# A graph layer on one core: edge attributes laid out by attribute, the first filter layer as two row-tiled matmuls, its bias on ACT

## The chip, the cores and the metric

One core of a Trainium2 chip. Times are device microseconds (us) of one execution; the kernel before is given as the median of three runs. Engine names are those of the profile: PE (TensorE, with PEld for its weight loads), DVE (VectorE), ACT (ScalarE), POOL (GpSimd), SP (SyncE, which here only starts transfers).

## The reference

A message-passing layer over 6250 nodes of 128 features and 200,000 edges sorted by `dst`, each edge with 20 attributes and one cutoff:

```python
h = jnp.maximum(_layernorm(x, axis=-1), 0.0)
xw = h @ W_in
W_ij = shifted_softplus(edge_attr @ W_f1 + b_f1) @ W_f2 + b_f2      # 200000 x 128
x_ij = xw[dst] * (W_ij * cutoff)
out  = segment_sum(x_ij, src, 6250)
x + shifted_softplus(out @ W_o1 + b_o1) @ W_o2 + b_o2
```

All of it is float32; `shifted_softplus(z)` is `softplus(z) - log 2`. In the reference, `src` picks the row that a message is added to and `dst` the row that is gathered.

## The kernel before

**Three stages.** A setup (to 146 us) normalizes the nodes, multiplies them by `W_in`, stores the product in three bf16-exact parts, turns the edge lists into the forms that the loop needs, and decides by two measured maxima which of two loops runs. Here that is the "hybrid" one. The edge loop (146 to about 2535 us) runs over 391 chunks of 512 edges. A last stage (about 100 us) adds up accumulators and computes the output layers. The change touches setup and loop.

**One chunk of the loop.** The 512 edges of a chunk are 4 tiles (T) of 128.

1. SP loads the chunk's attributes (128 partitions of 4 edges x 20 numbers), its row of `dst`, its row of `src`, and a window of 42 node rows (`xwin`). Each has four buffers.
2. PE transposes the attributes (line 1283) into `ps[0]`, and ACT copies them to `attrT` (line 756), whose row 80 is all ones.
3. PE multiplies with four copies of `W_f1`, each placed at the 20 rows of one tile with `b_f1` as row 81 and zeros elsewhere: four matmuls of 128 columns (line 1288, `hidden_product`) into `hidden_ps`, one PSUM bank.
4. ACT computes Abs, Exp and Ln (lines 719, 721, 723, `softplus`), DVE adds max(z, 0) (line 1026, `combine`), which signals `s_h`, hidden ready.
5. PE gathers the node rows by a one-hot product (line 1351); ACT scales them by the cutoff (line 749); PE runs the second filter layer (lines 1293, 1295); DVE multiplies the two into the message (line 1082).
6. The messages are added to nodes in one of two ways. In a turn of 16 chunks, chunks 3, 7, 11 and 15 are "on PE": their messages are put in 16 bins by 8 groups of four matmuls (`bin_up`, line 1316), each group emptied from one PSUM bank by ACT (`take_binned`, line 732) before the next may start, and later added by 48 half-height matmuls (`add_nodes`, line 1331). The other 12 are "pool chunks": PE sums equal `src` within a tile (`same_product`, line 1302), ACT empties the four sums (line 765), DVE makes targets (lines 1017, 1021), and POOL starts four adding scatters (line 606).

**What sets the order.** Every engine runs its queue in the order written; `hybrid_steps` calls each engine's `step(u, k)` for k = 0 to 15 of turn u. In step k, PE does: hidden(k+1); the first of two `bin_up` groups; gather and filter of chunk k; the transpose for k+2; in two steps of four `add_nodes` (`DENSE_AT`); the other `bin_up`; the sums of chunk k-1. ACT does: softplus(k+1); the first `take_binned`; the four scalings of k; the `attrT` copy for k+2; the other `take_binned`; the sums of k-1. `BINNED_AT` spreads the 8 groups of a PE chunk over the following steps, two in each step. So there are three kinds of step, by k mod 4: 1 and 3 ("plain": sums and no `add_nodes`), 2 (both) and 0 (`add_nodes` and no sums, since chunk k-1 was on PE).

Waits that matter here: hidden(k+1) waits for `attrT` and for hidden(k) ready; `bin_up` waits for the `take_binned` before it; the sums wait for the `attrT` copy, because both use `ps[0]`.

**Setup.** The edge lists are loaded as 391 rows of 512 integers, `cutoff` as floats. POOL casts `src` and `dst` to float (line 586) and `src` to int16 with the order of its elements changed (line 589). PE turns `src` and `cutoff` into columns by 32 transposes (line 1234, `column`), which ACT copies to `src_col` and `cut_col` (line 681). They stand ahead of the node blocks in PE's queue (`tr`, line 1210; `product`, line 1220). SP stores the parts (line 480) and clears the accumulators between them (line 464).

## Time and profile before

| | us |
|---|---|
| median of 3 runs (lowest to highest) | 2643.63 (2637.69 to 2644.58) |
| the profiled execution | 2637.52 |
| its span | 2635.6 |
| busy in the span: PE, PEld | 2334.9 (89%), 1729.0 (66%) |
| busy in the span: DVE, ACT, POOL | 1842.1 (70%), 1721.8 (65%), 1914.4 (73%) |
| mean granted TensorE clock | 0.968 of full speed |

The busy time of an engine is the union of its instructions. A matmul's record lasts longer than the time until the next matmul may start, so in a timeline the distance from one group's start to the next group's start is what the group costs, and the group's own length is when its result is there. A float32 matmul shows as two records ("x8" is four matmuls).

### The profile page before, as it was taken

To read this page: it belongs to the slowest core of one execution; us is meant where nothing else is said; L and a number is where in the kernel's file an instruction comes from. 1 tells how busy PE (TensorE), PEld (TensorE's weight loads), DVE (VectorE), ACT (ScalarE), POOL (GpSimd) and SP (SyncE) were. 2 spreads that over 40 slices of the span, in tenths; PEclk is the share of its full clock that TensorE was granted. 3 is DMA by queue.
4 is the path that set the end of the run, shared out by engine and by line. 5 is a ranking of instruction groups with operands and counts; after the bars stand their busy time and mean duration, and the time that the engine had idled before them with its cause. 6 is when DMAs were issued, how large, how long until landed. Compare 5 with 4: busy or idle time off the path is not lost.

```text
span 2635.6 us, 71554 instructions
## 1 busy us (share of the span) xinstructions
PE 2334.9 (89%) x19063; PEld 1729.0 (66%) x19063; DVE 1842.1 (70%) x4064; ACT 1721.8 (65%) x4279; POOL 1914.4 (73%) x1235
## 2 busy tenths in 40 slices
PE   3369999999999999999999999999999999999946
PEld 2247776776766677676676676676776676777724
DVE  7546777776777677676777777776677677777658
ACT  2147777776677677676777777677676777777713
POOL 2038887777777777877777787787777777777753
PEclk8579999999999999999999999999999999999967
DMA  7646555655655555555555555555555655555565
GB/s 261 188 78 97 91 90 88 92 87 88 91 87 87 89 90 86 88 92 86 87 88 90 86 90 90 86 88 88 89 87 88 91 87 88 88 90 88 84 140 173
DMA packets 436508, 259.95 MB, mean 99 GB/s; under 512 B 90238, under 2 KB 430181, under 8 KB 436233
## 3 DMA queue, kind: packets, MB, share of 16 engines
q0 software_dynamic: 170976, 80.61, 33.2%
q1 hardware_dynamic: 264121, 176.39, 25.0%
q14 instruction: 243, 1.99, 0.3%
q8 instruction: 32, 0.52, 0.1%
q10 hardware_dynamic: 1136, 0.44, 0.1%
HBM read 153.24 MB, written 104.04 MB: 98 GB/s over the span
## 4 chain that ended last, share of the span: by engine, by line
PE 59%; ACT 17%; issue 11%; DVE 4%; DMA 4%; ACTq 2%; POOL 2%; SPq 1%; DVEq 0%; POOLq 0%
PE ps L1331 13%; PE ps L1316 12%; PE ps L1288 12%; PE ps L1302 11%; PE ps L1295 6%; ACT region L721 5%; ACT region L749 5%; ACT region L719 5%; DMA acc<-region,target 2%; ACT region L732 2%; PE ps L1351 2%; PE ps L1293 1%; POOL acc L606 1%; ACTq L749 1%; ACTq L323 1%
## 5 line engine op out<-in xcount | busy, mean ns | idle before, releaser
L606 POOL DMA_INDIRECT acc<-region,target x1180 | 1863.9, 1580 | 640.1 <-issue 303.7
L1316 PE MATMUL ps<-region 128*128 128x386 bf16 x3072 | 660.9, 336 | 59.9 <-ACT region L732 46.1
L732 ACT ACTIVATE region<-ps 128x386 bf16<-128x386 f32 x768 | 372.9, 486 | 272.7 <-PE ps L1316 267.6
L1026 DVE SCALAR_TENSOR_TENSOR region<-ps,region 128x512 f32<-128x512 f32 x391 | 270.2, 691 | 375.4 <-ACT region L723 311.0
L1316 PEld LDWEIGHTS ps<-region 128*128 128x128 bf16 x3072 | 268.1, 98 | 293.7 <-ACT region L732 86.6
L749 ACT ACTIVATE region<-ps,cut_col 128x128 f32<-128x128 f32 x1564 | 442.7, 372 | 0.0
L1331 PE MATMUL ps<-region 64*128 64x392 bf16 x4608 | 418.5, 328 | 11.9 <-DVE region L1107 11.9
L1288 PE MATMUL ps<-attrT,w_f 81*128 81x128 f32 x3128 | 417.8, 276 | 12.1 <-ACT attrT L756 9.4
L1295 PEld LDWEIGHTS ps<-w_f,region 128*128 128x128 f32 x3128 | 411.3, 192 | 11.2
L1295 PE MATMUL ps<-w_f,region 128*128 128x128 f32 x3128 | 412.4, 275 | 0.0
L1288 PEld LDWEIGHTS ps<-attrT,w_f 81*128 81x128 f32 x3128 | 386.4, 192 | 27.7 <-ACT attrT L756 22.2
L1302 PEld LDWEIGHTS ps<-region 128*128 128x128 f32 x2360 | 291.8, 190 | 156.0 <-issue 79.8
L1302 PE MATMUL ps<-region 128*128 128x129 f32 x2360 | 330.8, 282 | 69.9 <-ACT attrT L756 37.3
L765 ACT ACTIVATE region<-ps 128x516 f32<-128x516 f32 x295 | 177.1, 600 | 266.8 <-PE ps L1302 146.9
L1331 PEld LDWEIGHTS ps<-region 64*128 64x128 bf16 x4608 | 208.7, 94 | 182.5 <-issue 37.0
L719 ACT ACTIVATE region<-ps 128x512 f32<-128x512 f32 x391 | 233.5, 597 | 128.3 <-PE ps L1288 58.0
L1107 DVE TENSOR_SCALAR region<-counting,region 128x392 bf16<-128x392 f16 x768 | 272.8, 395 | 0.0
L723 ACT ACTIVATE region<-region 128x512 f32<-128x512 f32 x391 | 246.2, 630 | 12.4
L721 ACT ACTIVATE region<-region 128x512 f32<-128x512 f32 x391 | 246.2, 630 | 12.3
L1082 DVE TENSOR_TENSOR region<-ps,region 128x512 f32<-128x512 f32 x295 | 203.0, 688 | 36.7 <-ACT region L749 32.2
L1017 DVE TENSOR_SCALAR moved<-region,weight_limit,spare_row 128x4 f32<-128x4 f32 x295 | 86.4, 293 | 195.8 <-ACT region L765 129.5
L1010 DVE TENSOR_TENSOR region<-src_b,src_col 128x512 f32<-128x512 int16 x295 | 201.2, 682 | 0.0
(129 smaller groups left out, 1990.7 us busy)
## 6 DMA issues: line engine op xcount, KB each, us to landing
dst_b<-dst_rows SPq DMA_DIRECT2D x391, 128.0 KB
src_b<-src_rows SPq DMA_DIRECT2D x295, 128.0 KB
xwin<-xw_parts SPq DMA_DIRECT2D x391, 63.0 KB
acc<-region,target POOLq DMA_INDIRECT x1180
attr<-in_edge_attr_dram SPq DMA_DIRECT2D x391, 40.0 KB
acc<-region SPq DMA_DIRECT2D x20, 640.0 KB, 5.1
region<-acc SPq DMA_DIRECT2D x64, 192.0 KB, 3.5
xw_parts<-parts SPq DMA_DIRECT2D x36, 256.0 KB, 3.2
```

The costliest lines, as they stand in the source:

```text
L606: nc.gpsimd.indirect_dma_start(out=acc[t], out_offset=bass.IndirectOffsetOnAxis(ap=target[:, slot, t:t + 1], axis=0), in_=summed[:, slot, ...
L719: nc.scalar.activation(a, z, ACT.Abs).then_inc(steps[0], 1)
L721: nc.scalar.activation(a, a, ACT.Exp, scale=-1.0).then_inc(steps[1], 1)
L732: nc.scalar.activation(binned[:, h, j, :], binned_ps[:, 0:PC], ACT.Copy).then_inc(s_binned, 1)
L749: last = nc.scalar.activation(xg[:, n % 2, t * F:(t + 1) * F], ps[3][:, t * F:(t + 1) * F], ACT.Copy, scale=cut_col[:, bass.ds(u * U + n, ...
L1026: V.scalar_tensor_tensor(hidden[:, odd, :], hidden_ps, 0.0, hidden_exp[:, odd, :], ALU.max, ALU.add).then_inc(s_h, 1)
L1107: V.tensor_scalar(in_node[:, i, slot, :], counting[:, 0:NL], binned[:, slot, j, 3 * F:3 * F + 1], binned[:, slot, j, 3 * F + 1:PC], ALU.su ...
L1288: ins = MM(hidden_ps[:, t * P:(t + 1) * P], w_f1[:, t, :], attrT[0:KA + 1, odd, :], start=True, stop=True)
L1295: ins = MM(ps[2][:, t * F:(t + 1) * F], hidden[:, odd, t * P:(t + 1) * P], w_f2[:, :], start=False, stop=(t == T - 1), skip_group_check=True)
L1302: ins = MM(sums_ps[:, t // 2, t % 2 * FW:(t % 2 + 1) * FW], same[:, odd, t * P:(t + 1) * P], message[:, odd, t, :], start=True, stop=True)
L1316: ins = MM(binned_ps[:, 0:PC], place[:, h % 2, t, j * P:(j + 1) * P], payload_high[:, h % 2, t, :], start=(t == 0), stop=(t == T - 1))
L1331: ins = MM(ps[6 + r][:, 0:NL], binned[rows, slot, j, part * F:(part + 1) * F], in_node[rows, i, slot, :], start=(d == ages[0] and part == ...
```

## The change

`edge_attr` reaches the chip as `(391, 2, 20, 256)`: for each chunk and each half of it, 20 rows of 256 edges. The loop loads it in two transfers, rows 0 to 19 and rows 64 to 83 of one buffer, and multiplies it from there. The transpose and the `attrT` copy are gone. The first filter layer is two matmuls of 256 columns, one on rows 0 to 19, one on rows 64 to 83, into two PSUM banks (4 and 5). The bias comes in by ACT's Abs (`bias=`) and DVE's `combine`; the constant that this leaves is added to the second layer's bias.

Bank 5 now holds half of the hidden layer and the fourth of the sums; the other three sums lie in bank 0 and the binned group moves to bank 1. So the fourth sum's matmul waits for hidden(k+1) to be ready, ACT empties the sums in two instructions, the fourth first, and hidden(k+2) waits for that first one. In PE's queue the first `bin_up` of a step is moved ahead of hidden(k+1).

`src` and `cutoff` also come as columns; `dst`, `src` are laid out so that an edge's place in a chunk is tile by tile, and the copies that changed the order become plain ones. The 200,000 edges are padded to 391 chunks (the last edge repeated with cutoff 0) in place of a last chunk that overlapped.

PE's queue in the loop, from the filter of a step with k mod 4 = 3 to the hidden product of the next. Names: `attrT_ready` is the `attrT` copy, `hidden_ready` `combine`, `binned_ready` `take_binned`, `sums_ready` the emptied sums. Before:

```order
L1293 MATMUL ps<-bf_parts,ones_bf 128x512 [waits message_ready,hidden_ready]
L1295 MATMUL ps<-w_f,region 128x128 x4
L1283 MATMUL ps<-ident,attr 80x128 [waits sums_ready,attrT_ready,attr_loaded1]
L1316 MATMUL ps<-region 128x386 [waits binned_ready,places_ready,payload_ready]
L1316 MATMUL ps<-region 128x386 x3
L1302 MATMUL ps<-region 128x129 [waits sums_ready,attrT_ready,message_ready,same_ready]
L1302 MATMUL ps<-region 128x129 x3
L1288 MATMUL ps<-attrT,w_f 128x128 [waits hidden_ready,attrT_ready]
L1288 MATMUL ps<-attrT,w_f 128x128 x3
L1316 MATMUL ps<-region 128x386 [waits binned_ready]
L1316 MATMUL ps<-region 128x386 x3
```

The same place after (L1236, L1238 filter; L1259 `bin_up`; L1245 sums; L1231 hidden):

```order
L1236 MATMUL ps<-bf_parts,ones_bf 128x512 [waits message_ready,hidden_ready]
L1238 MATMUL ps<-w_f,region 128x128 x4
L1259 MATMUL ps<-region 128x386 [waits binned_ready,places_ready_odd,payload_ready]
L1259 MATMUL ps<-region 128x386 x3
L1245 MATMUL ps<-region 128x129 [waits sums_ready,message_ready,same_ready]
L1245 MATMUL ps<-region 128x129 x2
L1245 MATMUL ps<-region 128x129 [waits hidden_ready]
L1259 MATMUL ps<-region 128x386 [waits binned_ready]
L1259 MATMUL ps<-region 128x386 x3
L1231 MATMUL ps<-attrT,w_f 128x256 [waits last_sums_ready,hidden_ready,attr_loaded1]
L1231 MATMUL ps<-attrT,w_f 128x256
```

The transpose is gone, the sums no longer wait for an `attrT` copy, and a `bin_up` group that stood behind the hidden product stands ahead of it, with a new wait (`last_sums_ready`) on the hidden product.

ACT's queue over the end of a plain step before (L756 `attrT`, L732 `take_binned`, L765 sums, L719 Abs of the next step):

```order
L749 ACTIVATE region<-ps,cut_col 128x128 x3
L756 ACTIVATE attrT<-ps 80x128 [waits hidden_in_psum,attrT_in_psum]
L732 ACTIVATE region<-ps 128x386 [waits binned_in_psum]
L765 ACTIVATE region<-ps 128x516 [waits scattered2,scattered3,scattered1,moved_ready,scattered0,sums_in_psum]
L719 ACTIVATE region<-ps 128x512 [waits hidden_ready,hidden_in_psum]
```

and after:

```order
L728 ACTIVATE region<-ps,cut_col 128x128 x3
L711 ACTIVATE region<-ps 128x386 [waits binned_in_psum]
L701 ACTIVATE region<-ps 128x129 [waits scattered2,scattered3,scattered1,moved_ready,scattered0,sums_in_psum]
L702 ACTIVATE region<-ps 128x387
L693 ACTIVATE region<-ps,bf 128x512 [waits hidden_ready,hidden_in_psum]
```

One instruction is gone from every step and one is added where there are sums.

The diff, cut to its core (the second, "general" loop is changed in the same way and does not run here):

```diff
+    NCH, HALVES, RBF, HALF = attr_cols.shape
-        w_f1 = sb("w_f1", [KA + 1, T, F])
+        w_f1 = sb("w_f1", [64 + RBF, F])
+        attrT = sb("attrT", [64 + RBF, 4, CE // 2])
-        attrT = sb("attrT", [96, 2, P])
-        attrT_ps, hidden_ps = ps[0], ps[4]
-        sums_ps = ps_all[:, 0:2, P:P + 2 * FW]
-        binned_ps = ps[5]
+        hidden_ps = ps_all[:, 4:6, 0:CE // 2]
+        sums_ps = [ps[0][:, t * FW:(t + 1) * FW] for t in range(T - 1)] + [ps[5][:, CE // 2:CE // 2 + FW]]
+        binned_ps = ps[1]
...
+            sp.dma_start(src_int, src_cols).then_inc(s_cols, 16)
+            sp.dma_start(cut_col[:, :, :], cutoff_cols).then_inc(s_cut, 16)
+            def load_attr(c, slot):
+                for r in range(2):
+                    sp.dma_start(attrT[64 * r:64 * r + RBF, slot, :],
+                                 attr_cols[bass.ds(c, 1), r, :, :].rearrange("o k e -> k (o e)")).then_inc(s_attr[slot], 16)
...
-                        after(sp, s_aTp, u, n - 4)
+                        after(sp, s_hp, u, n - 4)
                         sp.sem_inc(s_sp_go, 1)
-                        sp.dma_start(attr[:, slot, :], edge_rows(c).rearrange("(p t) k -> p (t k)", t=T)).then_inc(s_attr[slot], 16)
+                        load_attr(c, slot)
...
-                to_float(0, g).then_inc(s_chf, 1)
+                nc.gpsimd.tensor_copy(dst_f[0:rows_of[g], g, :], chunk_i[0:rows_of[g], 1, g, :]).then_inc(s_chf, 1)
-                to_16_bits(0, g).then_inc(s_src16, 1)
+                nc.gpsimd.tensor_copy(src_16[0:rows_of[g], g, :], chunk_i[0:rows_of[g], 0, g, :]).then_inc(s_src16, 1)
+            pool.wait_ge(s_cols, 16)
+            nc.gpsimd.tensor_copy(src_col[:, :, :], src_int).then_inc(s_col, 1)
...
-            for j in range(2 * G):
-                column(j)
...
+                nc.scalar.activation(a, z, ACT.Abs, bias=bias).then_inc(steps[0], 1)
+            def take_sums(slot):
+                nc.scalar.activation(summed[:, slot, T - 1, :], sums_ps[T - 1], ACT.Copy).then_inc(s_last_sum, 1)
+                nc.scalar.activation(summed[:, slot, 0:T - 1, :].rearrange("p t c -> p (t c)"), ps[0][:, 0:(T - 1) * FW], ACT.Copy).then_inc(s_s, 1)
...
-                        nc.scalar.activation(attrT[0:KA, n % 2, :], attrT_ps[0:KA, 0:P], ACT.Copy).then_inc(s_aT, 1)
...
-                    V.tensor_scalar(dst_rel[0:r, g, :].rearrange("c (t p) -> c p t", t=T), chunk_f[0:r, 1, g, :].rearrange("c (p t) -> c p t", t=T),
-                                    dst_min[0:r, g:g + 1], None, ALU.subtract).then_inc(s_rel, 1)
+                    V.tensor_scalar(dst_rel[0:r, g, :], dst_f[0:r, g, :], dst_min[0:r, g:g + 1], None, ALU.subtract).then_inc(s_rel, 1)
...
+                V.scalar_tensor_tensor(halves(hidden[:, odd, :]), hidden_ps, bf1_negative[:, 0:1], halves(hidden_exp[:, odd, :]),
+                                       ALU.max, ALU.add).then_inc(s_h, 1)
...
+            def hidden_product(slot):
+                for r in range(2):
+                    rows = slice(64 * r, 64 * r + RBF)
+                    ins = MM(hidden_ps[:, r, :], w_f1[rows, :], attrT[rows, slot, :], start=True, stop=True)
...
             def hybrid_products():
                 def step(u, k):
-                    n = k + 1
-                    if exists(u, n):
-                        after(pe, s_aT, u, n)
-                        after(pe, s_h, u, n - 1)
-                        hidden_product(n % 2)
                     jobs = binnings(u, k)
                     for job in jobs[:1]:
                         bin_up(*job)
+                    n = k + 1
+                    if exists(u, n):
+                        after_slot(pe, s_attr, u, n, 2)
+                        after(pe, s_h, u, n - 1)
+                        wait(pe, s_last_sum, pool_until(u, n - 3))
+                        hidden_product(n % 4)
...
-                        transposed_attr(n % 4)
...
-                        if exists(u, n + 3):
-                            after(pe, s_aT, u, n + 3)
-                        same_product(n % 2)
+                        same_product(n % 2, range(T - 1))
+                        if exists(u, n + 2):
+                            after(pe, s_h, u, n + 2)
+                        same_product(n % 2, (T - 1,)).then_inc(s_sp, 1)
...
+        "edge_attr_20": attr.reshape(chunks, 2, CE // 2, rbf).transpose(0, 1, 3, 2),
```

## Rows read from the trace of the kernel before

**Rows 1.** Busy time by stretch; columns in the first row.

```profile
core 0: us, PE busy (x) PEld busy (x) DVE busy (x) ACT busy (x) POOL busy (x), PEclk, DMA share, GB/s
1000.00:1500.00 500.00, 472.71 (x3953) 350.49 (x3954) 353.69 (x784) 352.87 (x886) 389.87 (x247) 1.00 0.58 89
```

**Rows 2.** Group of the scatters: xcount, busy us, mean ns, idle before, releasers.

```profile
L606 POOL DMA_INDIRECT acc<-region,target x1180 | 1863.9, 1580 | 640.1 <-issue 303.7 <-DVE target L1021 298.7 <-DMA acc<-region,target 26.8
```

**Rows 3.** PE's timeline, four steps of the loop: start us, us, operation, xcount, idle.

```profile
1220.53 1.06 PE L1288 MATMUL ps<-attrT,w_f 81*128 81x128 f32 x8
...
1227.36 1.06 PE L1288 MATMUL ps<-attrT,w_f 81*128 81x128 f32 x8
...
1230.81 0.86 PE L1316 MATMUL ps<-region 128*128 128x386 bf16 x4 [0.25 <-ACT region L732]
1231.98 1.16 PE L1302 MATMUL ps<-region 128*128 128x129 f32 x8 [0.31 <-issue]
1232.97 1.05 PE L1288 MATMUL ps<-attrT,w_f 81*128 81x128 f32 x8
1233.87 0.86 PE L1316 MATMUL ps<-region 128*128 128x386 bf16 x4
1234.56 0.40 PE L1351 MATMUL ps<-xwin,onehot 126*128 126x128 bf16 x4
...
1235.91 0.27 PE L1283 MATMUL ps<-ident,attr 128*80 128x128 f32 x1
1236.11 2.17 PE L1331 MATMUL ps<-region 64*128 64x392 bf16 x24
1238.21 0.86 PE L1316 MATMUL ps<-region 128*128 128x386 bf16 x4
1238.91 1.05 PE L1288 MATMUL ps<-attrT,w_f 81*128 81x128 f32 x8
...
1244.53 1.06 PE L1288 MATMUL ps<-attrT,w_f 81*128 81x128 f32 x8
```

**Rows 4.** ACT's timeline in the same steps.

```profile
1228.45 0.60 ACT L719 ACTIVATE region<-ps 128x512 f32<-128x512 f32 x1
...
1230.28 0.47 ACT L732 ACTIVATE region<-ps 128x386 bf16<-128x386 f32 x1
...
1231.64 0.28 ACT L756 ACTIVATE attrT<-ps 80x128 f32<-80x128 f32 x1
1231.80 0.50 ACT L732 ACTIVATE region<-ps 128x386 bf16<-128x386 f32 x1
1233.41 0.60 ACT L765 ACTIVATE region<-ps 128x516 f32<-128x516 f32 x1 [1.11 <-PE ps L1302]
1234.07 0.60 ACT L719 ACTIVATE region<-ps 128x512 f32<-128x512 f32 x1
...
1239.11 0.49 ACT L732 ACTIVATE region<-ps 128x386 bf16<-128x386 f32 x1 [1.57 <-PE ps L1316]
```

**Rows 5.** Timeline of the setup, all engines.

```profile
21.64 2.28 POOL L586 CAST region<-region 128x512 f32<-128x512 int32 x4 [5.57 <-DMA region<-in_dst_dram]
...
23.87 9.28 POOL L589 CAST region<-region 128x512 int16<-128x512 int32 x4
...
25.62 7.58 DVE L861 TENSOR_SCALAR std<-meanvar 128x49 f32<-128x49 f32 x1
...
36.57 4.19 DVE L884 TENSOR_SCALAR region<-region,meanvar,rstd 128x128 f32<-128x128 f32 x16
...
40.90 1.97 PE L1210 MATMUL ps<-ident,region 128*128 128x128 f32 x8
...
45.43 1.82 SPq L480 DMA_DIRECT2D xw_parts<-parts  x3
...
59.68 4.75 DVE L925 TENSOR_SCALAR region<-region,dst_min 128x512 bf16<-128x512 f32 x4
```

**Rows 6.** SP's timeline in the loop: one start of an attribute load.

```profile
1222.96 0.35 SPq L519 DMA_DIRECT2D attr<-in_edge_attr_dram  x1
```

More of the change, by code:

```diff
@@ L288, in gnn_kernel, with halves @@
         quads_stored = [len(range(h, NQ, 2)) for h in range(2)]
-        ndma = sum(1 for g in range(G) if min(rows_of[g], NCH - 1 - g * P) > 0) + 1
+        def halves(columns):
+            return columns.rearrange("p (r c) -> p r c", r=2)
         def known(c):
@@ L715, in _, with softplus @@
                     whole(q - 1)
-            def softplus(z, a, steps, value):
-                nc.scalar.activation(a, z, ACT.Abs).then_inc(steps[0], 1)
+            def softplus(z, bias, a, steps, value):
+                nc.scalar.activation(a, z, ACT.Abs, bias=bias).then_inc(steps[0], 1)
                 act.wait_ge(steps[0], value)
@@ L934, in bins @@
             def bins():
[L936 removed]
+                dve.wait_ge(s_cols, 16)
                 dve.wait_ge(s_src16, G)
@@ L1261, in ranks @@
                 ins.then_inc(s_rkps, 1)
-            pe.wait_ge(s_w, 16 * (7 + 2 * T))
+            pe.wait_ge(s_w, 16 * 10)
             pe.wait_ge(s_shift, 1)
-            MM(ps[6][:, 0:F], ones[:, :], w_f2[:, :], start=True, stop=True)
+            MM(ps[6][:, 0:F], bf1_less_ln2[:, :], w_f2[:, :], start=True, stop=True)
             MM(ps[6][:, F:2 * F], bo1_less_ln2[:, :], w_o2[:, :], start=True, stop=True).then_inc(s_bias, 1)
-            for j in range(2 * G):
-                column(j)
             for q in range(NQ + 1):
@@ L1279, in _ @@
             TR(ps[7][0:1, 0:P], rank_max[:, 0:1], ident[:, :]).then_inc(s_rmps, 1)
[L1281 to L1288 removed]
+            def hidden_product(slot):
+                for r in range(2):
+                    rows = slice(64 * r, 64 * r + RBF)
+                    ins = MM(hidden_ps[:, r, :], w_f1[rows, :], attrT[rows, slot, :], start=True, stop=True)
                 ins.then_inc(s_hp, 1)
@@ L1297, in filter_product, with same_product @@
                 ins.then_inc(s_fp, 1)
-            def same_product(odd):
-                for t in range(T):
-                    ins = MM(sums_ps[:, t // 2, t % 2 * FW:(t % 2 + 1) * FW], same[:, odd, t * P:(t + 1) * P], message[:, odd, t, :], start=True, stop=True)
-                ins.then_inc(s_sp, 1)
+            def same_product(odd, tiles):
+                for t in tiles:
+                    ins = MM(sums_ps[t], same[:, odd, t * P:(t + 1) * P], message[:, odd, t, :], start=True, stop=True)
+                return ins
             payload_high = payload.rearrange("p h t c -> p (h t c)").bitcast(bf16).rearrange(
@@ L1442, with rows, columns @@
     from concourse.bass_utils import run_bass_kernel_spmd as _run
+    src, dst = _np.asarray(inputs["src"]), _np.asarray(inputs["dst"])
+    edge_attr, cutoff = _np.asarray(inputs["edge_attr_20"]), _np.asarray(inputs["edge_weight1"])
+    edges, rbf = edge_attr.shape
+    chunks = -(-edges // CE)
+    spare = chunks * CE - edges
+    def rows(a, mode):
+        return _np.pad(a.reshape(edges), (0, spare), mode=mode).reshape(chunks, CE)
+    def columns(a):
+        return a.reshape(chunks, T, P).transpose(2, 0, 1)
+    attr = _np.pad(edge_attr, ((0, spare), (0, 0)))
+    laid = {
+        "x": _np.asarray(inputs["x"]),
+        "src": rows(src, "edge"),
+        "src_cols": columns(rows(src, "edge")),
+        "dst": rows(dst, "edge"),
+        "dst_cols": columns(rows(dst, "edge")),
+        "edge_attr_20": attr.reshape(chunks, 2, CE // 2, rbf).transpose(0, 1, 3, 2),
+        "edge_weight1": columns(rows(cutoff, "constant")),
+    }
+    for name in _WEIGHTS:
+        laid[name] = _np.asarray(inputs[name])
     nc = _bacc.Bacc("TRN2", target_bir_lowering=False, num_devices=1)
     arrays, args = {}, []
-    for name in _INS:
-        a = _np.ascontiguousarray(inputs[name])
+    for name, a in laid.items():
+        a = _np.ascontiguousarray(a)
         arrays[f"in_{name}_dram"] = a
```

185 lines of the change are left out of this document (56 added, 129 removed).

## The prediction

> **What bounds the kernel now.** I read the busy time by stretch first. In a stretch of the edge loop PE is busy 473 of 500 us at the full granted clock (1.00, the level of 2.4 GHz), ACT and DVE about 353, POOL 390 [rows 1]. POOL looks free but is not: between two scatters it stands about 0.30 us for issue (303.7 us over 965 gaps), so one scatter costs 1.58 + 0.31 = 1.89 us and twelve pool chunks of four take 91 us of the 97 that a turn of 16 chunks takes. Of its idle time 299 us is waiting for DVE's targets [rows 2]. So PE's path is what ends last, and POOL would allow 6% at most.
>
> Then the two timelines, side by side. From one hidden product to the next I read four step lengths: 6.83 us (`add_nodes` and sums), 5.61 (plain), 5.94 (`add_nodes`, no sums), 5.62 (plain); together 24.00 us for four chunks [rows 3]. The reader is to see that PE is not simply full. In a plain step it stands twice, 0.25 us for `take_binned` and 0.31 us for the `attrT` copy [rows 3]. The loop that sets a plain step's length is a ring through two engines: hidden product, softplus, `take_binned`, `bin_up` or `attrT`, sums, hidden product. Only in the steps with `add_nodes` is it PE's own work. An operation taken from PE is worth its time only if it stands in that ring.
>
> **The hidden product itself.** Before: eight records of 128 columns, 0.90 us from its start to the next group's [rows 3]. After: two matmuls of 256 columns, so four records (a float32 matmul is two) of 0.213 us each, since a record of 128 columns takes 0.90 / 8 = 0.112 us and twice the columns take twice that, a fixed part less. One after the other that is 0.86 us, the same work. All gain lies in overlap. The trace has overlap on half-height matmuls: the 24 of line 1331, 392 columns each, take 2.10 us [rows 3], 0.175 a pair, where a full-height matmul of 386 columns takes 0.69 / 4 = 0.17 alone. But they are issued in turn, upper half, lower half. Here both records of the first matmul come before both of the second. In order, the second record of the first has to wait for its own rows; then the first record of the second matmul can run beside it. That is three units, 0.64 us. Bounds: two units 0.43, four units 0.86. I take 0.64.
>
> The Trainium skill says, in "TensorE: Matmul & The Clock Gate", section "Step-by-step: what each phase is for", that weight loads are pulled ahead but matmuls stay in program order; no run here shows it for this pattern. By it the sum would be the three units that I take. Its "TensorEngine Tiling (Array Packing)", section "Theoretical Speedup", promises up to 4x for a contraction of 32 or less; by it the two matmuls overlap fully, which is rival B.
>
> Going over to matmuls of another height costs something. A transpose of one record is followed by line 1331 after 0.20 us [rows 3], where one float32 record takes 0.112: 0.09 for the change. Line 1331's 2.10 us hold 12 pairs at 0.163 (392 columns at 2.4 GHz) = 1.96, so leaving costs at most 0.14. I take 0.09 for entering and 0.09 for leaving the hidden product's height; below, nothing.
>
> **A plain step after.** From the start of the hidden product: result and Abs start 0.64 + 0.16 + 0.05 = 0.85 (the 0.21 is how far Abs at 1234.07 lies behind eight records from 1232.97 [rows 3, 4]). From Abs to the first `take_binned` is 1.83, and PE may start `bin_up` 2.36 after Abs (1230.81 against 1228.45): 3.21. `bin_up` 0.70: 3.91. Sums 0.90: 4.81. Now the other `bin_up`, which before stood behind the hidden product: the `take_binned` it waits for comes where the `attrT` copy stood, 3.19 after Abs, and takes 0.50: 4.54, so no wait; 5.51. The hidden product also waits for the fourth sum: from sums to ACT's start is 1.43 in the row, 1.33 without the start after a stall, then the 0.28 of a small copy (the `attrT` copy's size) and 0.05: 3.91 + 1.66 = 5.57. Entering 0.09: 5.66 against 5.61. The removed wait of 0.31, and the shorter product, are used up by a `bin_up` of 0.70 in the ring.
>
> **The step with `add_nodes` and no sums.** Hidden 0.64, leaving 0.09, gather and filter 1.35 (1234.56 to 1235.91) = 2.08, entering 0.09, `add_nodes` 2.10: 4.27. `bin_up` starts; ACT begins to empty it 0.90 later (1239.11 against 1238.21) and needs 0.49 + 0.05: 5.71 [rows 3, 4]. Before, the hidden product filled this time; now the next `bin_up` stands here and has to wait. It takes 0.70: 6.41, entering 6.50 against 5.94, a new wait of some 0.7 us.
>
> **The step with both.** 4.27, `bin_up` 4.97, sums 5.87, `bin_up` 6.57; fourth sum 4.97 + 1.66 = 6.63, entering 6.72 against 6.83. Here the transpose and the records saved on PE count.
>
> **Sum of the loop.** 5.66 + 6.50 + 5.66 + 6.72 = 24.54 against 24.00: 0.54 us later per four chunks. `bin_up` runs from chunk 7 on, (391 - 7) / 4 = 96 groups: +52 us.
>
> **What costs nothing.** ACT loses a copy of 0.28 in every step and gains about 0.2 in twelve of sixteen (two instructions for one, a start-up more); it waits for PE 1.1 us before the sums in a plain step [rows 4]. The second attribute transfer costs SP one more issue of 0.35 us per chunk [rows 6]; it is hidden by the loads running several steps ahead of PE (four buffers each); were it not, it would cost 0.35 x 391 = 137 us. Abs and `combine` with a bias operand and two banks: taken as unchanged, at worst 0.03 each, 0.06 x 391 = 23 us, as they stand in the ring. POOL stays under its 22.7 us per four chunks.
>
> **The setup.** POOL's reordering cast of `src` takes 9.28 us, and DVE's line 861, an operation on 49 numbers, lasts 7.58 us and ends just when that cast ends (33.2) [rows 5]. After, the four casts are plain, as the ones at 21.64 (2.28 us), then one of 1564 elements, three times 512, about 1.8. POOL ends at 23.9 + 2.3 + 1.8 = 28.0, and line 861 with it: 5.2 earlier. Normalizing starts at 36.6 and its first quarter takes 1.1, but PE begins with the nodes only at 40.9, behind the column transposes; after, at 31.4 + 1.1 = 32.5: 8.4 us earlier, and SP's first store (45.4, idle before) with it. DVE's line 925 (4.75 us) becomes plain and takes about half: 2.3. The first chunk saves its transpose and copy, 0.6. Together 11 us; bounds 0 (if the stores' transfers, not their start, set the pace) and 14.
>
> **Total.** 2637.5 (this execution, 1.9 above its span) + 52 - 11 = 2678.5. The median of the runs is 6 us above this execution; I put 2680. A change under 0.3%, some 8 us, cannot be told from none here.
>
> **The rivals.**
> - A, the forecast: three units, both changes of height, the new wait. 2680; own range 2655 to 2710, from leaving and entering at 0 to 0.14 in single places and from the 23 us above. Chance 0.52.
> - B, faster: the two matmuls overlap fully, two units. Each of four steps loses 0.21: 0.84 x 96 = 81 us. 2678 - 81 = 2597. For it: the pairs of line 1331. Against: their order. It decides for faster once the product falls under 0.64 - 0.54 / 4 = 0.50 us. Chance 0.20.
> - C: no overlap for float32 records, four units. +0.22 x 4 x 96 = 84: 2763. For it: the trace has overlap in bf16 only. Chance 0.15.
> - D: matmuls of 20 rows need no change of height on either side (the 0.09 entering in all four steps, leaving in the two with `add_nodes`: 0.54). The loop keeps its 24.0 and the setup's 11 us remain: 2627 to 2643. Against: the 0.20 us at line 1331. Chance 0.13.
>
> A plain counter-argument, that PE is the busiest engine and gets two operations less, would give up to (0.11 + 0.26) x 391 = 145 us; the steps above say why it does not come.
>
> **The numbers.** Range: from B, 2592, through A, without most of C: 2740. Faster by over 0.3%: B and half of D, 0.27. Within: the rest of D and A's edge, 0.08. Slower: 0.65.
>
> **What would show it.** In the profile after: the hidden product as four records with starts 0, 0.21, 0.21 and 0.43 (A), in two pairs (B), or 0.21 apart throughout (C). A wait of about 0.7 us for `take_binned` ahead of the first `bin_up` behind `add_nodes`, step lengths of 5.66, 6.50, 5.66 and 6.72, POOL waiting longer for targets, and line 861 short with the loop starting near 135 us. Wrong would be: step lengths under 24.0 in sum with the product at 0.64, or PE waiting for attributes.

## The result and the profile after

The changed kernel takes 2691.22 us (median of 4 runs, 2690.46 to 2691.66) against 2640.74 (4 runs, 2637.69 to 2644.58): a ratio of 1.019, 95% interval 1.0172 to 1.0208. It is slower by 50 us. In the profiled executions the spans are 2689.4 and 2635.6 us, 53.8 apart; the mean granted clock is 0.958 against 0.968.

The window of the middle of the loop, against [rows 1]:

```profile
core 0: us, PE busy (x) PEld busy (x) DVE busy (x) ACT busy (x) POOL busy (x), PEclk, DMA share, GB/s
1000.00:1500.00 500.00, 437.61 (x3433) 287.57 (x3432) 347.25 (x760) 344.32 (x836) 378.53 (x240) 0.99 0.56 86
```

PE has 35 us less to do in 500, and every other engine is less busy too, because all of them go slower; the granted clock is 0.99 here, where it was 1.00. Nothing has become the bound by its busy time; something waits. The groups of instructions of after say what (columns as in [rows 2]):

```profile
L592 POOL DMA_INDIRECT acc<-region,target x1180 | 1865.1, 1581 | 698.1 <-DVE target L985 377.2
L1259 PE MATMUL ps<-region 128*128 128x386 bf16 x3072 | 667.8, 339 | 291.6 <-ACT region L711 255.3
L990 DVE SCALAR_TENSOR_TENSOR region<-ps,bf_negative,region 128x512 f32<-128x512 f32 x391 | 293.7, 751 | 496.2 <-ACT region L697 396.2
L693 ACT ACTIVATE region<-ps,bf 128x512 f32<-128x512 f32 x391 | 268.6, 687 | 420.1 <-PE ps L1231 288.3
```

Line 1259 is `bin_up`, line 711 `take_binned`: PE now stands 292 us before `bin_up`, 255 of it for line 711; in the trace before it is 60 and 46. POOL waits longer for its targets, 377 against 299 [rows 2]. Line 693 is Abs and line 990 `combine`, both with the bias operand: 687 and 751 ns, where before they took 597 and 691.

PE's timeline, which answers to [rows 3]. It starts at the end of the step in which the loop's code turns back to its start; a plain step, a step with both and, after the second gap, the regular step without sums follow (line 1231 is the hidden product, 1295 the gather, 1245 the sums, 1274 `add_nodes`):

```profile
1233.91 0.86 PE L1259 MATMUL ps<-region 128*128 128x386 bf16 x4 [0.68 <-ACT region L711]
1234.70 0.70 PE L1231 MATMUL ps<-attrT,w_f 20*128 20x256 f32 x4
...
1237.90 0.86 PE L1259 MATMUL ps<-region 128*128 128x386 bf16 x4 [1.05 <-ACT region L711]
1238.60 1.05 PE L1245 MATMUL ps<-region 128*128 128x129 f32 x8
1239.49 0.85 PE L1259 MATMUL ps<-region 128*128 128x386 bf16 x4
1240.37 0.70 PE L1231 MATMUL ps<-attrT,w_f 20*128 20x256 f32 x4
1241.00 0.40 PE L1295 MATMUL ps<-xwin,onehot 126*128 126x128 bf16 x4
...
1242.44 2.17 PE L1274 MATMUL ps<-region 64*128 64x392 bf16 x24
1244.54 0.86 PE L1259 MATMUL ps<-region 128*128 128x386 bf16 x4
1245.24 1.05 PE L1245 MATMUL ps<-region 128*128 128x129 f32 x8
...
1256.83 0.86 PE L1259 MATMUL ps<-region 128*128 128x386 bf16 x4
1258.28 0.86 PE L1259 MATMUL ps<-region 128*128 128x386 bf16 x4 [0.59 <-ACT region L711]
1259.07 0.70 PE L1231 MATMUL ps<-attrT,w_f 20*128 20x256 f32 x4
```

The reader is to see three things. The product takes 0.63 us to the next group (1240.37 to 1241.00), where it took 0.90 [rows 3]. Two groups of `bin_up` now stand in the plain step between one hidden product and the next (1237.90, 1239.49). And PE waits for `take_binned`: 1.05 us in the plain step, where it was 0.25 [rows 3], and 0.59 us between the two groups of the step without sums (1258.28; 0.68 at the turn, 1233.91).

ACT's timeline in the plain step, against [rows 4]:

```profile
1235.45 0.69 ACT L693 ACTIVATE region<-ps,bf 128x512 f32<-128x512 f32 x1 [1.60 <-PE ps L1231]
...
1241.11 0.69 ACT L693 ACTIVATE region<-ps,bf 128x512 f32<-128x512 f32 x1 [0.50 <-PE ps L1231]
```

Abs starts 0.75 after the product does (1234.70, 1235.45), and 5.66 us from one Abs to the next.

**Where the 54 us are.** I took the starts of all 391 Abs operations. To the first one: 151.1 us before, 139.3 after, so 11.8 less. Chunks 0 to 32: 178.9 and 179.5. The 21 turns from chunk 32 to 368: 2040.1 and 2105.2, 65.1 more. The rest: 265.6 and 265.4. Within the turns, medians of the 21, from one Abs to the next:

| step | before | after |
|---|---|---|
| plain (two in four) | 5.62 | 5.65 |
| `add_nodes`, no sums | 5.94 | 6.43 |
| both | 6.82 | 6.63 |
| four chunks | 24.00 | 24.36 |
| the two steps at the loop's turn | 7.98 + 4.72 | 8.33 + 5.53 |
| odd ones: chunk 7 to 8, 9 to 10 | 6.82, 5.94 | 6.91, 6.52 |
| mean turn of 16 | 97.15 | 100.25 |

The regular steps give 0.36 x 4 = 1.4 of the 3.1 us that a turn grew by; the rest is around the turn, in the odd steps, and in eight longer turns.

**The longer turns and the clock.** Of the 21 turns of after, 8 take 101.83 us in the mean and 12 take 99.39; one, at chunk 32, has no turning back in it and takes 97.84. The eight are just those in which the granted clock falls to half, the level of 1.2 GHz, for a stretch right behind PE's waits at the turn. One of them, first the windows, then PE's timeline:

```profile
1030.00:1033.70 3.70, 1.50 (x8) 0.62 (x8) 2.55 (x6) 2.95 (x8) 3.09 (x3) 1.00 0.59 67
1033.70:1040.50 6.80, 6.80 (x31) 5.19 (x30) 5.22 (x11) 3.85 (x9) 3.65 (x3) 0.50 0.59 84
```

```profile
1031.52 0.86 PE L1259 MATMUL ps<-region 128*128 128x386 bf16 x4 [1.79 <-ACT region L711]
1033.06 0.94 PE L1259 MATMUL ps<-region 128*128 128x386 bf16 x4 [0.68 <-ACT region L711]
1033.94 1.22 PE L1231 MATMUL ps<-attrT,w_f 20*128 20x256 f32 x4
1035.09 0.60 PE L1295 MATMUL ps<-xwin,onehot 126*128 126x128 bf16 x4
```

The product takes 1.15 us to the next group here, at the full clock 0.63. In before the clock stays at 1.00 in all 21 turns. So of the 65 us, 8 x 2.4 = 20 are the clock's, and 2.2 us a turn (99.39 against 97.2), some 46 us, are there at the full clock. Why the clock falls in eight turns and not in the others stays open: in the turn from 1222 us PE waits as long (1.80 and 0.68 us) and the clock stays at 1.00.

### The profile page after: what moved, and what is told of

Its sections match the earlier page's. It is cut to its first block, busy times and chain, and to the rows that moved or that the text cites. A ratio compares the mean times of both kernels' runs of the same rounds, so it can differ in the third digit from the quotient of the medians.

```text
span 2689.4 us, 67669 instructions
## 1 busy us (share of the span) xinstructions
PE 2225.5 (83%) x17076; PEld 1469.1 (55%) x17076; DVE 1857.7 (69%) x4064; ACT 1728.8 (64%) x4175; POOL 1907.3 (71%) x1231
## 4 chain that ended last, share of the span: by engine, by line
PE 43%; ACT 16%; issue 15%; DMA 11%; DVE 9%; POOL 2%; SPq 1%; ACTq 1%; DVEq 1%; POOLq 0%
PE ps L1259 14%; DMA acc<-region,target 9%; PE ps L1274 9%; PE ps L1245 6%; PE ps L1231 6%; PE ps L1238 5%; ACT region L693 4%; ACT region L695 4%; ACT region L711 3%; PE ps L1295 2%; POOL acc L592 1%; ACT region L702 1%; ACT region L728 1%; DVE region L1072 1%; PE ps L1236 1%
## 5 line engine op out<-in xcount | busy, mean ns | idle before, releaser
L1259 PE MATMUL ps<-region 128*128 128x386 bf16 x3072 | 667.8, 339 | 291.6 <-ACT region L711 255.3
L990 DVE SCALAR_TENSOR_TENSOR region<-ps,bf_negative,region 128x512 f32<-128x512 f32 x391 | 293.7, 751 | 496.2 <-ACT region L697 396.2
L1259 PEld LDWEIGHTS ps<-region 128*128 128x128 bf16 x3072 | 254.9, 97 | 550.8 <-ACT region L711 318.7
L693 ACT ACTIVATE region<-ps,bf 128x512 f32<-128x512 f32 x391 | 268.6, 687 | 420.1 <-PE ps L1231 288.3
L1238 PEld LDWEIGHTS ps<-w_f,region 128*128 128x128 f32 x3128 | 422.5, 196 | 11.9
L1238 PE MATMUL ps<-w_f,region 128*128 128x128 f32 x3128 | 423.2, 279 | 0.0
L1245 PEld LDWEIGHTS ps<-region 128*128 128x128 f32 x2360 | 312.5, 195 | 25.0 <-DVE region L990 1.9
L1245 PE MATMUL ps<-region 128*128 128x129 f32 x2360 | 318.1, 278 | 1.7 <-DVE region L990 1.5
L1231 PE MATMUL ps<-attrT,w_f 20*128 20x256 f32 x1564 | 281.3, 432 | 17.1 <-DMA attrT<-in_edge_attr_dram 5.1
L1231 PEld LDWEIGHTS ps<-attrT,w_f 20*128 20x128 f32 x1564 | 126.5, 187 | 159.4 <-issue 150.6
L1001 DVE TENSOR_SCALAR region<-counting,place_col 128x1024 bf16<-128x1024 f16 x384 | 196.8, 533 | 0.0
L701 ACT ACTIVATE region<-ps 128x129 f32<-128x129 f32 x295 | 81.9, 278 | 173.2 <-DMA acc<-region,target 123.5
```

Source lines behind the costliest of these rows:

```text
L693: nc.scalar.activation(a, z, ACT.Abs, bias=bias).then_inc(steps[0], 1)
L990: V.scalar_tensor_tensor(halves(hidden[:, odd, :]), hidden_ps, bf1_negative[:, 0:1], halves(hidden_exp[:, odd, :]), ALU.max, ALU.add).then ...
L1231: ins = MM(hidden_ps[:, r, :], w_f1[rows, :], attrT[rows, slot, :], start=True, stop=True)
L1238: ins = MM(ps[2][:, t * F:(t + 1) * F], hidden[:, odd, t * P:(t + 1) * P], w_f2[:, :], start=False, stop=(t == T - 1), skip_group_check=True)
L1245: ins = MM(sums_ps[t], same[:, odd, t * P:(t + 1) * P], message[:, odd, t, :], start=True, stop=True)
L1259: ins = MM(binned_ps[:, 0:PC], place[:, h % 2, t, j * P:(j + 1) * P], payload_high[:, h % 2, t, :], start=(t == 0), stop=(t == T - 1))
```

## The experiments

All ratios are to runs of the kernel before on the same chip (2637.9 us for runs 1 to 4, 2638.6 for 5 and 9, 2638.1 for 6 to 8, 2640.4 for 10).

**1. The order of PE's queue.** From after:

```diff
-                    jobs = binnings(u, k)
-                    for job in jobs[:1]:
-                        bin_up(*job)
                     n = k + 1
                     ...
                         hidden_product(n % 4)
+                    jobs = binnings(u, k)
+                    for job in jobs[:1]:
+                        bin_up(*job)
```

> The changed kernel with the first binning group of each step back behind the hidden product. Theory 1 (the displaced group and its wait for take_binned in the ring made the change slower): the step without sums falls from 6.43 to about 5.2 us, since the hidden product no longer waits behind two emptied groups; plain steps stay near 5.6, now held by the fourth sum's way through ACT (1.66 us after the sums start, where the displaced group had hidden it); the step with both rises to about 7.3. Sum 23.6 against 24.35 us per four chunks: 2691 - 70 = about 2620 us. Theory 2 (the longer Abs and combine cost it): order is of no account, 2691. Theory 3 (the fourth sum's wait decides in every step): no step gets shorter, 2691 or more.

Measured: 2651.15 us, 1.0041 (1.0027 to 1.0055); steps 5.65, 5.67, 5.65, 7.33; at the turn 8.33 and 3.99; mean turn 98.5. PE's timeline: the end of a step with both (to 1223.67), then, behind the gap, a step without sums (1229.32 to 1234.98) and a plain one (to 1240.63):

```profile
1223.67 0.70 PE L1231 MATMUL ps<-attrT,w_f 20*128 20x256 f32 x4 [0.70 <-issue]
...
1229.32 0.70 PE L1231 MATMUL ps<-attrT,w_f 20*128 20x256 f32 x4 [0.71 <-ACT region L701]
...
1234.98 0.70 PE L1231 MATMUL ps<-attrT,w_f 20*128 20x256 f32 x4
...
1240.63 0.70 PE L1231 MATMUL ps<-attrT,w_f 20*128 20x256 f32 x4 [0.70 <-ACT region L701]
```

Line 701 is the emptying of the fourth sum, which shares a bank with half of the hidden product. The step without sums falls from 6.43 to 5.67, so its wait was the displaced `bin_up`'s. But where there are sums, the hidden product now comes sooner than the fourth sum's place is free, and stands 0.70 us; the step with both grows from 6.63 to 7.33 (its wait, at 1223.67, is put down to issue, but it lies as far behind the sums as the other two). Over four chunks that is 24.30 against 24.36: nothing. What is gained lies at the turn: its second step takes 3.99 against 5.53. A turn has four steps with both and only three other steps without sums, so over a turn at the full clock 1.0 of the 1.5 us is left (98.41 against 99.39), some 22 us. The clock gives most of the rest: it falls in 2 of the 21 turns, for 3.4 us each, where it fell in 8 for 6.8; that is 16 us. My expectation of 2620 had the wait and the step with both right, but put the step without sums at 5.2 us, 0.5 short, and left the turn and the clock out.

**2. The bias operand.** Abs and `combine` with no per-partition operand, which leaves `b_f1` out of the hidden layer; everything else as in after:

```diff
-                nc.scalar.activation(a, z, ACT.Abs, bias=bias).then_inc(steps[0], 1)
+                nc.scalar.activation(a, z, ACT.Abs).then_inc(steps[0], 1)
...
-                V.scalar_tensor_tensor(halves(hidden[:, odd, :]), hidden_ps, bf1_negative[:, 0:1], halves(hidden_exp[:, odd, :]),
+                V.scalar_tensor_tensor(halves(hidden[:, odd, :]), hidden_ps, 0.0, halves(hidden_exp[:, odd, :]),
```

> The changed kernel with Abs and combine without the bias operand (Abs of the product alone, max with 0), so b_f1 is left out of the hidden layer. If the operand makes Abs 0.69 in place of 0.60 us and combine 0.75 in place of 0.69: both fall back, the three steps of four whose ring runs through ACT lose 0.09 each, 0.27 x 96 = 26 us: about 2665. Theory 2, both in the ring in all steps: 0.15 x 391 = 59 us, 2632. If reading from two PSUM banks is the cause: 0.69 and 0.75 stay, 2691.

Measured: 2661.09 us, 1.0084 (1.0067 to 1.0101), 30 us under after and near the 2665 expected. The two groups:

```profile
L990 DVE SCALAR_TENSOR_TENSOR region<-ps,region 128x512 f32<-128x512 f32 x391 | 270.5, 692 | 458.4 <-ACT region L697 277.1
L693 ACT ACTIVATE region<-ps 128x512 f32<-128x512 f32 x391 | 233.5, 597 | 415.2 <-PE ps L1231 228.6
```

Both still read two banks, and both are back at their durations of before. So the 0.09 and 0.06 us are the operand's, not the banks'. The plain step falls from 5.65 to 5.55 and the turn's second from 5.53 to 5.44; the step with both and the one without sums stay at 6.63 and 6.43. So the operand is in the ring of half the steps, not of three in four as the expectation had it. That is some 0.7 us a turn at the full clock (98.72 against 99.39), 15 us; the clock falls in 4 turns instead of 8, some 11 us more. The total near 2665 is in part luck.

**3. The same rows.** Both halves of the product on rows 0 to 19; nothing can run side by side:

```diff
-                    rows = slice(64 * r, 64 * r + RBF)
-                    ins = MM(hidden_ps[:, r, :], w_f1[rows, :], attrT[rows, slot, :], ...)
+                    ins = MM(hidden_ps[:, r, :], w_f1[0:RBF, :], attrT[0:RBF, slot, r, :], ...)
```

> The changed kernel with both halves of the attributes on rows 0 to 19, so that the two hidden matmuls use the same rows; all else (height, banks, waits, two transfers) stays. If the records of the two matmuls overlap fully, as their starts in pairs say: four records of 0.213 us follow one another, 0.86 + 0.09 to the next group in place of 0.63: +0.32 x 4 x 96 = 123 us, about 2814. If the weight loads and not the overlap set the 0.63: stays at 0.63, 2691. As the prediction had it (three units, in order): 0.64 to 0.86, +0.22 x 384 = 84 us, 2775.

Measured: 2829.43 us, 1.0723 (1.0704 to 1.0742), 138 us over after. PE's timeline (line 1230 is the product here):

```profile
1240.87 1.12 PE L1230 MATMUL ps<-attrT,w_f 20*128 20x256 f32 x4
1241.93 0.40 PE L1294 MATMUL ps<-xwin,onehot 126*128 126x128 bf16 x4
```

1.06 us to the next group here, 1.03 as the median of 391 products, 0.63 in after. The starts of the four records (medians) are 0, 0.29, 0.51, 0.72 here and 0, 0.007, 0.29, 0.33 in after. So in after they run in two pairs; a record is 0.216 (0.51 to 0.72). Four of them one by one are 0.86, two pairs 0.43, and 0.17 and 0.20 are on top: nearly the same in both kernels, so it belongs to a product of 20 rows among matmuls of 128 and not to the overlap, 0.075 of it behind the first record (0.29 less 0.216), the rest behind the last. The step grows by 0.40, not by the 0.32 expected; 0.40 x 4 x 96 = 154 us would come, but the clock falls in 2 turns here and in 8 in after, which gives some 15 back.

**4. The layout alone.** The kernel before, with the attributes laid out as 80 x 128 per chunk, loaded straight into `attrT`. The transpose and its copy are gone; the product of eight records, the banks and the order stay:

```diff
-                sp.dma_start(attr[:, slot, :], edge_rows(c).rearrange("(p t) k -> p (t k)", t=T))
+                sp.dma_start(attrT[0:KA, slot, :], edge_attr[bass.ds(c, 1), :, :].rearrange("o k e -> k (o e)"))
```

> The kernel before with one part of the change: the attributes come laid out as the 80 rows by 128 edges that attrT held, loaded straight into it (one transfer), no transpose and no attrT copy. Hidden product (four full-height matmuls with the bias row), banks, Abs, the order of the groups and the setup stay as before. Theory 1: plain steps lose the 0.31 us wait and the copy, 5.62 to about 5.1; the other two lose the transpose, 5.94 to 5.84 and 6.83 to 6.73; sum 22.8 us per four chunks, just above POOL's 22.7: 2641 - 115 = about 2526. Rival (the transpose and copy were hidden anyway, and only the rest of the change counts): 2630 to 2641.

Measured: 2519.61 us, 0.9555 (0.9539 to 0.9571), 6 under the expectation. The hidden products:

```profile
1219.06 1.05 PE L1268 MATMUL ps<-attrT,w_f 81*128 81x128 f32 x8
...
1224.10 1.05 PE L1268 MATMUL ps<-attrT,w_f 81*128 81x128 f32 x8
...
1229.92 1.05 PE L1268 MATMUL ps<-attrT,w_f 81*128 81x128 f32 x8
...
1234.96 1.06 PE L1268 MATMUL ps<-attrT,w_f 81*128 81x128 f32 x8
```

Steps of 5.04, 5.82 and 5.04 us, with a product 0.27 longer than after's. The removal of the transpose and its copy is worth 118 us; the rest of the change spends that, the setup's gain, and 50 more.

**5. The setup alone.** After's tables and casts, before's loop.

> The setup of the changed kernel (columns, plain casts and copies, padded chunks) with the loop of before (transpose, attrT copy, four matmuls with the bias row, old banks and order). By the prediction's term: 11 us less than before, 2638 - 11 = 2627. If the stores' transfers set the setup's pace and not their start: 2638. The loop's step lengths stay 5.62, 5.94, 5.62 and 6.83.

Measured: 2733.32 us, 1.0363 (1.0349 to 1.0377). A miss by 106 us. The first Abs comes at 140.7, 10.4 earlier than before, and the regular steps are 5.62, 5.94, 5.62, 6.82 as in before. But the two steps at the turn take 10.52 and 7.55 instead of 7.98 and 4.72. PE's timeline at a turn (line 1259 is the sums here, 1245 the hidden product), then the queue q8:

```profile
1239.65 1.16 PE L1259 MATMUL ps<-region 128*128 128x129 f32 x8 [0.32 <-ACT attrT L737]
1244.32 2.07 PE L1245 MATMUL ps<-attrT,w_f 81*128 81x128 f32 x8 [3.51 <-issue]
```

```profile
q8 instruction: 213, 3.49, 0.5%
```

PE stands 3.5 us on nothing that the profile names, and one of the queues that carry instructions moved 3.49 MB, in before 0.52. That pointed to where the loop's code lies, which the next three runs test. The hidden product's 2.07 us is twice its usual 1.05, and the window says why:

```profile
1242.70:1249.50 6.80, 5.18 (x23) 4.33 (x24) 1.92 (x5) 3.01 (x8) 5.58 (x5) 0.50 0.45 45
```

Behind the stand the granted clock is at half, in 20 of the 21 turns. From this product to `add_nodes` it is 5.69 us, where the shifted kernel of run 6, at the full clock, takes 3.13. So 2.6 us of what a turn loses is the clock's, which fell behind PE's stand.

**6. to 8. The code shifted.** Three kernels get 64 waits on PE ahead of the loop in place of one, 63 instructions more that do nothing:

```diff
+            for _ in range(64):
                 pe.wait_ge(s_rmax, 1)
```

> The setup of after with the loop of before, and 64 more instructions of TensorE ahead of the loop, each a wait for a semaphore that has already reached its value; they do nothing but move the loop's code to another address. Theory of placement: the 10.5 and 7.6 us around the loop's turn (before: 8.0 and 4.7), with TensorE idle there on nothing that the profile names and 3.49 MB on queue q8 against 0.52, come from where the loop's code lies. The shift changes it: turn back to about 97.2 us, total near 2627 us (2637 less the 11 of the setup), plus 1 to 4 us for the 64 waits. Rival: the 5.4 us a turn belong to what the setup leaves behind, the layout of buffers or the order of loads, and not to addresses of code: 2733 us again.

> The kernel before with the same 64 waits of TensorE ahead of the loop. Theory of placement: the turn of the loop may cost more than in before or as much, by where the code comes to lie: 2640 us if this shift crosses no boundary, about 2740 if it does. Rival (placement is without effect): 2638 to 2642 us.

> After with the same 64 waits of TensorE ahead of the loop. It asks whether the 8.33 and 5.53 us around its turn (before: 7.98 and 4.72), and with them some 14 to 25 us of its 50, come from placement. If they come from the order of the work, as the other steps do: 2691 to 2695 us. If from placement: anything from 2670 to 2790 us, with the change in the two steps around the turn alone.

Measured: setup alone shifted 2628.97 us, 0.9964 (0.995 to 0.9979), 104 under the same kernel unshifted; before shifted 2642.26, 1.0014 (1.0005 to 1.0024); after shifted 2688.92, 1.0193 (1.0176 to 1.021). In the first the turn's steps are 7.91 and 4.72 again and its queue q8 reads

```profile
q8 instruction: 32, 0.52, 0.1%
```

The shift takes away the whole of the miss, with the stand of 3.5 us, the fall of the clock and the 3 MB. That it acts by where the code lies is the reading that fits the queue's bytes; no row shows the addresses. The waits put the first Abs back by 4.5 us (145.2 against 140.7), by 3.6 in before and by 2.0 in after. Between the two shifted kernels, which both pay them, the first Abs comes 9.5 us earlier (154.7, 145.2); the medians are 13.3 apart, but the runs of before shifted lie between 2638.5 and 2644.4, so the other 4 are no gain of the setup that could be shown. And after keeps its 8.29 and 5.53 at the turn when shifted, and its q8 moves 0.48 MB in both: nothing in it points to this cause.

**9. One full product.** After's setup and layout as 20 x 512, but one full-height matmul of 512 columns on 65 rows (the attributes, zeros, the bias row), before's banks and order, no bias operand:

```diff
-                for r in range(2):
-                    rows = slice(64 * r, 64 * r + RBF)
-                    ins = MM(hidden_ps[:, r, :], w_f1[rows, :], attrT[rows, slot, :], ...)
+                MM(hidden_ps, w_f1[:, :], attrT[:, slot, :], start=True, stop=True).then_inc(s_hp, 1)
```

> The version that the runs point to: the setup of the changed kernel, the attributes as 20 rows by 512 edges in one transfer, and the first filter layer as one full-height matmul of 512 columns on 65 rows (20 of weights, zeros, the bias on row 64 against a row of ones), so no change of height, one bank, Abs without a bias operand, and the banks, sums and order of before. Against the layout alone (2520): the setup takes 11 us off, and the product two records of 0.427 us, 0.86 in place of 0.90, off the two steps that are PE's own work, 0.04 x 2 x 96 = 8: about 2501. Rival: POOL now sets the end (twelve scatters of 1.89 us in four chunks are 22.7 us, the steps of the layout alone sum to 22.6): then only the setup's 11 us come, 2509.

Measured: 2486.11 us, 0.9425 (0.9412 to 0.9438), 15 under the expectation and the fastest of all.

```profile
1224.65 1.02 PE L1225 MATMUL ps<-attrT,w_f 65*128 65x512 f32 x2
1225.51 0.85 PE L1252 MATMUL ps<-region 128*128 128x386 bf16 x4
...
1229.66 1.02 PE L1225 MATMUL ps<-attrT,w_f 65*128 65x512 f32 x2
```

The product takes 0.86 us to the next group, 0.23 more than after's, and the step is 5.01, 0.64 less: no fourth sum in the product's bank, no `bin_up` ahead of it, no operand, no change of height. These four go together here. Runs 1 and 2 price the order and the operand alone; of the fourth sum's bank there is only the wait of 0.70 us that run 1 lays bare, and no run puts it back alone.

**10. Two loads.** The same, with its attribute load in two:

```diff
+                for r in range(2):
+                    half = slice(r * CE // 2, (r + 1) * CE // 2)
                     sp.dma_start(attrT[0:RBF, slot, half], ...)
```

> The version with one full-height product per chunk (2486 us), its attribute load split in two of 256 columns each, so 782 starts on SP instead of 391 and nothing else changed. In after some steps are longer than the order of the work gives: 6.91 and 6.52 in the middle of a turn where the same steps elsewhere take 6.63 and 6.43, and 8.33 and 5.53 around the turn against 7.98 and 4.72; together 1.0 us a turn, and 101 packets more on the instruction queue q14. Theory: the second load a chunk makes SP's code longer, which has to be fetched in every turn: q14 near 344 packets, turn 91.1 to about 92.1 us, 2486 to some 2508. Rival: the odd steps belong to PE's order in after, and the second load only costs SP time that is hidden: q14 may rise, but the steps stay 5.01, 6.68, 5.01, 5.79 and the total 2484 to 2490.

Measured: 2500.05 us, 0.9469 (0.9456 to 0.9482), 14 over the one with a single load, or 12 with each taken against before on its own chip; first step at the turn 8.21 against 7.82, all regular and middle steps unchanged, q14 with 343 packets (242 with one load, 344 in after). So the second transfer is not free: it costs some 0.4 us at each turn, and some more in single places. The same step of after is 0.35 over before's (8.33 against 7.98), which fits; but run 4, with one load, has 8.12 there, so in after the share of the load is not shown. The odd steps in after's middle do not come from it. For one of them after's own ACT timeline names the wait, the copy of the fourth sum standing for a scatter that still reads the buffer it fills:

```profile
1271.21 0.28 ACT L701 ACTIVATE region<-ps 128x129 f32<-128x129 f32 x1 [0.83 <-DMA acc<-region,target]
```

## Why the prediction was right, step by step

The forecast was 2680 us and the time is 2691; the direction, the new wait and the setup's gain came out. That the number is so near is in part luck: the product was 0.10 us too long in the sum and Abs 0.09 too short, the steady steps cost 35 us and not 52, and 30 us that the sum did not have, two thirds of them the clock's, filled most of the gap.

**The product: near in total, wrong in mechanism.** I had three units of 0.213 in order and 0.09 for leaving, 0.73 us to the next group. The records start in two pairs, as rival B had it, so 0.43; the change of height costs not 0.09 but 0.20 within the product. Together 0.63. The 0.09 before it held (`bin_up` at 1233.91 to the product at 1234.70 is 0.79, `bin_up` at 1244.54 to the sums 0.70). Rival B's overlap is real, most of its gain is not: the full product of run 9 pays 0.86 and neither change of height, so the two row-tiled halves save 0.86 - 0.72 = 0.14 us on PE. The Trainium skill's "TensorEngine Tiling (Array Packing)", section "Key Properties", says that changing the tiling mode drains TensorE; the trace shows no drain as such, but it agrees that a change is not free: 0.09 + 0.20 us a time. Its "Theoretical Speedup" counts without that price.

**The ring.** "A `bin_up` of 0.70 in the ring" held: the plain step was to be 5.66 and is 5.65. Two errors cancelled. The product is 0.10 shorter than I had it, and Abs is 0.09 longer: the term that failed is "Abs and `combine` with a bias operand and two banks: taken as unchanged, at worst 0.03 each". They are 0.09 and 0.06 longer, and without the operand the kernel is 30 us faster (run 2), where I had 23 as the worst; about 11 of the 30 come by the clock. The Trainium skill states it, in "ScalarE: Activation LUTs", section "What ACT_TABLE_LOAD costs": each per-partition pointer operand adds about 93 ns. The trace agrees, with 90; my sum had left it out.

**The new wait.** 0.7 us were forecast for `take_binned` in the step with `add_nodes` and no sums, 6.50 in all; the step is 6.43, with a wait of 0.59, and 5.67 when the order is undone (run 1). The step with both was to be 6.72 and is 6.63, the product's 0.10 again. Four chunks: 24.54 forecast, 24.36 measured, so 35 us in 96 groups, not 52.

**What the sum lacked.** I multiplied four regular steps by 96 and passed over the loop's turn. There the displaced `bin_up` costs most: ACT stands 3.28 us for its next instructions, `take_binned` comes late, and PE with two `bin_up` ahead of the hidden product has nothing else to run. PE's and ACT's timelines at a turn of after, then the stand of ACT in before, which is shorter:

```profile
1228.40 2.16 PE L1274 MATMUL ps<-region 64*128 64x392 bf16 x24
1232.37 0.86 PE L1259 MATMUL ps<-region 128*128 128x386 bf16 x4 [1.80 <-ACT region L711]
```

```profile
1229.92 0.69 ACT L693 ACTIVATE region<-ps,bf 128x512 f32<-128x512 f32 x1 [3.28 <-issue]
...
1231.84 0.47 ACT L711 ACTIVATE region<-ps 128x386 bf16<-128x386 f32 x1
```

```profile
1211.28 0.60 ACT L719 ACTIVATE region<-ps 128x512 f32<-128x512 f32 x1 [2.53 <-issue]
```

Behind these waits of PE the granted clock falls in 8 of 21 turns: 20 us of the loop's 65, and the largest thing that the sum did not have. The turn itself and the odd steps make the rest of what the regular steps leave. The second load, "hidden by the loads running several steps ahead", may be part of it: run 10 refutes that term for the turn, with 12 to 14 us in its kernel; in after it was not measured.

**The setup.** -11 forecast, -11.8 measured at the first Abs (-10.4 and -9.5 in the two pairs with before's loop). Its working held in the main, against [rows 5]:

```profile
27.14 1.48 POOL L586 CAST src_col<-region 128x1564 f32<-128x1564 int32 x1
27.77 0.90 DVE L829 TENSOR_SCALAR std<-meanvar 128x49 f32<-128x49 f32 x1
...
33.58 2.14 PE L1175 MATMUL ps<-ident,region 128*128 128x128 f32 x8 [7.75 <-DVE region L852]
...
37.96 2.63 SPq L474 DMA_DIRECT2D xw_parts<-parts  x3
...
52.22 1.66 DVE L893 TENSOR_SCALAR region<-region,dst_min 128x512 bf16<-128x512 f32 x4
```

POOL ends at 28.6 (28.0 forecast), the operation on 49 numbers with it and 0.90 long instead of 7.58, the nodes start at 33.6 (32.5), the first store at 38.0 instead of 45.4, so 7.4 us earlier and not 8.4; the plain form of the 4.75 us operation takes 1.66, less than the half I gave it, which in the forecast's own sum makes up for most of that.

**Rivals.** C (no overlap, 2763) falls with the pairs. D (no change of height) falls with the 0.17 and 0.20 us that a product of 20 rows has on top without and with overlap (run 3), and that the product on 65 rows has not (run 9: 0.86 for two records 0.43 apart). The counter-argument, up to 145 us for two operations less, was closer than I let it be: run 4 takes away just those two operations and gets 118. It is true of the layout and untrue of this kernel, which put a `bin_up`, a shared bank and an operand in the place that the copy left free.

## What to carry to other kernels

When an operation leaves a ring between two engines, see to it that nothing takes its place: here the transpose's removal was worth 118 us, and new banks, a new order, a bias operand and changes of height turned it into a loss of 50. Undoing the order gives back 40 us, leaving out the operand 30, both in part through the clock; the others were not measured one by one. Do the sum for the loop's turn as well as for its steady steps; an order that is neutral in the steady state can cost 1.5 us at every turn, where one engine comes late. Look at the granted clock turn by turn before calling a longer turn unexplained: a wait of PE that looks cheap can be followed by a stretch at half the clock. Row tiling pays only for what is left after two changes of height; if the whole contraction fits in one matmul with zeros between, measure that first. And when an edit outside a loop changes the loop's time, shift the code by some idle instructions and measure again.

## What the runs showed of the hardware

- The same kernel takes 2733 or 2629 us, by 63 idle instructions more on PE ahead of the loop; in the slow one a queue carries 3.49 MB of instructions instead of 0.52, and the turn's two steps take 18.1 us instead of 12.6.
- In that slow kernel PE stands 3.5 us at the turn and the granted clock is at half for 6.8 us behind it, in 20 of 21 turns; in after PE waits 1.8 and 0.7 us there and the clock falls in 8 of 21, at 2.4 us a turn; in before it never falls in these turns.
- Two float32 matmuls of 20 rows each, on rows 0 and 64, run in pairs of records, 7 ns apart, though each is two records and the whole first matmul is written ahead of the second. On the same rows their records run one by one, 0.216 us apart.
- A product of 20 rows among matmuls of 128 costs 0.09 us before it and 0.20 on top of its records; one on 65 rows costs neither.
- A per-partition bias operand adds 0.09 us to ACT's Abs of 128 x 512 (0.597 to 0.687) and 0.06 to DVE's operation with a scalar operand (0.692 to 0.751).
- A wait for a semaphore that is already reached costs PE about 0.056 us: with 63 more of them its idle time ahead of the next instruction grows from 3.45 to 6.91 us in before and from 3.44 to 7.03 in after.
